# Upward products of a mixture of experts on 32-row strips of the TensorE array

## The reference

```python
probs = softmax(einsum('bsd,de->bse', x, gate_w) + gate_b)
topk_vals, topk_idx = jax.lax.top_k(probs, 2)
mask = sum(one_hot(topk_idx, 4), axis=-2)
masked = probs * mask / (sum(probs * mask, axis=-1, keepdims=True) + 1e-09)
h = gelu(einsum('bsd,edh->ebsh', x, w1) + b1)      # 96 -> 384 units, 4 experts
y = einsum('ebsh,ehd->ebsd', h, w2) + b2           # 384 units -> 96
out = einsum('bse,ebsd->bsd', masked, y)
```

## Time and profile before

| what | value |
|---|---|
| runs shown | 1208.01, 1211.01, 1211.23 us; median 1211.01 |
| profiled execution, own time | 1204.52 us |
| its span, first to last instruction | 1202.7 us |
| around the span | 1.8 us |
| mean granted clock of TensorE | 0.962 of full |
| TensorE busy | 1083.8 us, 90% of the span |
| VectorE, ScalarE, GpSimd busy | 58%, 44%, 33% |
| experts' own part | from about 1045 us to the end |

### The profile page before, as it was taken

The page is one execution under the profiler, slowest core; times in us unless marked ns, Lnnn a source line. Parts: engine busy times, 40 slices in busy tenths (PEclk is TensorE's granted clock), DMA queues, the critical chain, the costliest instruction groups (busy, mean ns, idle before and its releaser), DMA issues. The chain is left out here.

```text
span 1202.7 us, 26997 instructions
## 1 busy us (share of the span) xinstructions
PE 1083.8 (90%) x10561; PEld 708.1 (59%) x10561; DVE 702.9 (58%) x2003; ACT 525.4 (44%) x855; POOL 395.2 (33%) x616
## 2 busy tenths in 40 slices
PE   5999988899989799999999996888888978899998
PEld 2677655577745567676666664455455444466665
DVE  3899734687734466666666666476455565443333
ACT  1666623466523333434343331454343422365654
POOL 4766553766364310110101111425000000336442
PEclk9999999899979899999999999888799999899999
DMA  6400000000000000000000000000000000000000
GB/s 124 88 2 2 2 2 0 1 1 2 1 1 1 1 1 1 1 2 1 1 1 1 1 1 1 1 1 2 2 2 1 2 2 2 1 8 15 9 15 14
DMA packets 28534, 9.50 MB, mean 8 GB/s; under 512 B 26689, under 2 KB 28416, under 8 KB 28416
## 3 DMA queue, kind: packets, MB, share of 16 engines
q1 hardware_dynamic: 25392, 6.95, 2.8%
q10 hardware_dynamic: 3024, 0.92, 0.4%
HBM read 6.29 MB, written 1.57 MB: 7 GB/s over the span
## 5 line engine op out<-in xcount | busy, mean ns | idle before, releaser
L164 POOL TENSOR_TENSOR ln_v<-MV,eps 128x2 f32<-128x2 f32 (+3 forms) x81 | 16.2, 200 | 407.9 <-PE bank L1141 244.7
L1203 ACT ACTIVATE fa_e<-bank 128x1024 f32<-128x1024 f32 x64 | 65.5, 1023 | 156.8 <-PE bank L1111 156.8
L1255 DVE TENSOR_REDUCE fa_z<-bank 128x4 f32<-128x1024 f32 x64 | 77.9, 1217 | 26.4 <-PE bank L1093 24.4
L137 PE MATMUL bank<-hT,e_w 96*64 96x512 f32 x384 | 91.0, 610 | 0.0
L2049 ACT ACTIVATE ex_G<-bank,e_b 128x512 f32<-128x512 f32 x96 | 64.4, 687 | 49.9 <-PE bank L137 47.2
L2121 DVE SCALAR_TENSOR_TENSOR X<-bank,ex_L,X 128x96 f32<-128x96 f32 x128 | 31.7, 310 | 91.5 <-PE bank L137 85.0
L1853 DVE TENSOR_REDUCE ca_z<-bank 128x2 f32<-128x256 f32 x96 | 48.9, 551 | 48.7 <-PE bank L1580 48.7
L137 PEld LDWEIGHTS bank<-e_w,ex_G 128*64 128x64 f32 x1536 | 67.0, 137 | 17.3 <-issue 10.6
L1111 PE MATMUL bank<-fa_a,fa_b 64*128 64x256 f32 x512 | 73.0, 404 | 1.1 <-DVE fa_a L1262 1.1
L1771 ACT ACTIVATE ca_e<-bank 128x768 f32<-128x768 f32 x48 | 38.9, 810 | 76.4 <-PE bank L1580 76.4
L167 POOL TENSOR_TENSOR ln_r<-ln_v,minus_half 128x2 f32<-128x2 f32 (+3 forms) x81 | 71.8, 886 | 0.0
(11 more groups left out here) (251 smaller groups left out, 2493.7 us busy)
## 6 DMA issues: line engine op xcount, KB each, us to landing
out_tokens<-X SPq DMA_DIRECT2D x8, 192.0 KB, 2.1
X<-in_x SPq DMA_DIRECT2D x14, 96.0 KB, 3.4
e_w<-in_L_ffn_w SPq DMA_DIRECT2D x2, 576.0 KB
bias0r<-in_L_conv_rpb_table ACTq DMA_DIRECT2D x16, 24.0 KB
m0w<-in_L_conv_mlp_w SPq DMA_DIRECT2D x2, 144.0 KB
m1w<-in_L_conv_w SPq DMA_DIRECT2D x2, 144.0 KB
f_w<-in_L_ffn_W SPq DMA_DIRECT2D x2, 142.5 KB
mixer<-in_mixer SPq DMA_DIRECT2D x1, 256.0 KB
```

Source lines behind the costliest of these rows:

```text
L137: last = pe.matmul(out[columns], weights[:, columns], moving, **flags)
L1203: act.activation(E[v % 2][:], k.banks[:, b:b + 2, :].rearrange("p i (c q) -> p i c q", c=2), ACT.Exp).then_inc(s["exp"], 1)
L1255: dve.tensor_reduce(Z[v % 2][:].rearrange("p c (i d) -> p i c d", i=2)[:, :, :, D2], k.banks[:, b:b + 2, :].rearrange("p i (c q) -> p i c ...
```

## The change

- Four chunks go up together (`up(n, i, slot)`, i = 0 to 2: a **quad**), each into its own bank. The contraction over 96 channels is cut into three strips of 32 rows. In each of three turns the four chunks use four strips of the array: chunks 0 to 2 of the quad take strips (b + turn) % 3 of rows 0 to 95, and chunk 3 the rows 96 to 127. The matmuls are 32 rows x 128 columns x 512 tokens, no longer halves.
- For chunk 3 the tokens are copied onto rows 96 to 127, three groups of 32 channels side by side (`HX`), by three DMAs per step on SP's queue (`fourth_strip`). HX lies in the feed-forward block's buffers `bf_H`, which now belong to `k.H`. The weights of each quad's fourth chunk are loaded a second time onto these rows (three DMAs more at the start).
- Within a bank, the matmul of a later turn waits for that of the turn before (`part0` to `part3`). A quad's first matmul waits for all gelus of the quad before, and for the copies.
- `G` is one buffer with eight slots; gelu and down go chunk by chunk. `down(n, i)` does a quad's four chunks one after the other, each for four token tiles.
- The order of TensorE and ScalarE goes by three quads instead of four experts. The second upward group inside causal attention is gone; its `yield` stays.

```diff
-        def up(n, e, slot):
-            for j in range(KH):
-                v = KH * e + j
-                after(pe, s["gelu"], UP * n + v + 1 - NB)
-                halves(pe, bank[v % NB], k.ew1[:, e, j * P:(j + 1) * P], k.hT[slot][:], start=True, stop=True).then_inc(s["up"], 1)
+        def up(n, i, slot):
+            pe.wait_ge(s["hT"], n + 1)
+            pe.wait_ge(s[f"hx{slot}"], 16 * KH * (n // 2 + 1))
+            after(pe, s["gelu"], UP * n + NB * i)
+            for turn in range(KH):
+                for b in range(NB):
+                    strip = (b + turn) % KH if b < KH else KH
+                    rows = slice(32 * strip, 32 * strip + 32)
+                    v = NB * i + b if b < KH else KH * i + turn
+                    moving = k.hT[slot][rows, :] if b < KH else HX[slot][rows, turn, :]
+                    if turn:
+                        pe.wait_ge(s[f"part{b}"], (KH - 1) * (QUADS * n + i) + turn)
+                    last = pe.matmul(bank[b][:], k.ew1[rows, v, :], moving, start=(turn == 0), stop=(turn == KH - 1), skip_group_check=True)
+                    last.then_inc(s["up"] if turn == KH - 1 else s[f"part{b}"], 1)
...
         for n, slot, first, last in order:
-            for e in range(EXPERTS):
...
+            for i in range(QUADS):
+                if not first or i:
+                    up(n, i, slot)
+                if i == first and not last:
+                    tokens(n + 1, 1 - slot)
+                if i:
+                    down(n, i - 1)
                 elif not first:
...
+                    down(n - 1, QUADS - 1)
+                if i == QUADS - 1 and not last:
                     gate(n + 1, 1 - slot)
...
+        def gelus(n, i):
+            v = UP * n + NB * i
+            for b in range(NB):
+                act.wait_ge(s["up"], v + b + 1)
+                after(act, s["down"], v + b - 7)
+                act.activation(G[:, (v + b) % 8, :], bank[b][:], ACT.Gelu, bias=k.eb1[:, (NB * i + b) // KH, (NB * i + b) % KH:(NB * i + b) % KH + 1]).then_inc(s["gelu"], 1)
...
+            for i in range(QUADS):
+                if not first or i:
+                    gelus(n, i)
+                if i == first and not last:
                     tokens(n + 1, 1 - slot)
-                if e == 2 + first and not last:
+                if i == 1 + first and not last:
                     exps(n + 1, 1 - slot)
...
+        def fourth_strip(n):
+            sp.wait_ge(s["hT"], n + 1)
+            after(sp, s["up"], UP * (n - 1))
+            for g in range(KH):
+                sp.dma_start(HX[n % 2][C:P, g, :], k.hT[n % 2][32 * g:32 * g + 32, :]).then_inc(s[f"hx{n % 2}"], 16)
```

More of the change, by code:

```diff
@@ L218 @@
 CA_SEMS = LN_SEMS + "init cmask pad T hT ab abe vt v sc nm zt aug st exp av otr rec nrm ote pj oc bt"
-EX_SEMS = LN_SEMS + "T hT gl gate exp up gelu down acc g3 g4 g5 st"
+EX_SEMS = LN_SEMS + "T hT hx0 hx1 gl gate exp part0 part1 part2 part3 up gelu down acc g3 g4 g5 st"
 def setup(k, bank, a):
@@ L337, in setup @@
     k.gb = row("b_gate", a["L3_ffn_gate_b"])
-    k.ew1 = weight("e_w1", [C, EXPERTS, HID], a["L3_ffn_w1"].rearrange("e c h -> c e h"))
+    k.ew1 = sb("e_w1", [P, EXPERTS * KH, P])
+    loads.append((k.ew1[0:C].rearrange("c (e j) h -> c e (j h)", e=EXPERTS), a["L3_ffn_w1"].rearrange("e c h -> c e h")))
+    for i in range(KH):
+        e, j = divmod(4 * i + 3, KH)
+        loads.append((k.ew1[C:P, KH * i:KH * i + KH, :], a["L3_ffn_w1"][e, :, j * P:(j + 1) * P].rearrange("(g p) h -> p g h", p=32)))
     k.eb1 = weight("e_b1", [P, EXPERTS, KH], a["L3_ffn_b1"].rearrange("e (k p) -> p e k", p=P))
@@ L1328, in binary_ffn @@
     hT = sb("hT", [C, GT * P])
-    H = [sb(f"H{i}", [P, KH, GT * P]) for i in range(2)]
+    H = k.H
     Z = sb("Z", [P, GT, C])
@@ L1930, in experts @@
     UP = EXPERTS * KH
+    QUADS = UP // NB
     def sb(name, shape, dt=F32):
@@ L1939, in experts @@
     tmp = [sb(f"tmp{i}", [P, 4, C]) for i in range(2)]
-    G = [sb(f"G{i}", [P, KH, 512]) for i in range(2)]
+    G = sb("G", [P, 8, 512])
+    HX = [t[:, :, 0:512] for t in k.H]
     full = [P, 4, EXPERTS]
@@ L1992, in gate, with down @@
             last.then_inc(s["gl"], 1)
-        def up(n, e, slot):
-            for j in range(KH):
-                v = KH * e + j
-                after(pe, s["gelu"], UP * n + v + 1 - NB)
-                halves(pe, bank[v % NB], k.ew1[:, e, j * P:(j + 1) * P], k.hT[slot][:], start=True, stop=True).then_inc(s["up"], 1)
[L2000 to L2008, removed]
+        def up(n, i, slot):
[12 more added lines that the diff above has]
+                    last.then_inc(s["up"] if turn == KH - 1 else s[f"part{b}"], 1)
+        def down(n, i):
+            for b in range(NB):
+                v = NB * i + b
+                e, j = divmod(v, KH)
+                u = EXPERTS * n + e
+                pe.wait_ge(s["gelu"], UP * n + v + 1)
+                if j == 0:
+                    after(pe, s["acc"], 4 * (u - 1))
+                for t in range(4):
+                    last = halves(pe, bank[4 + e % 2][:, t * C:(t + 1) * C], G[:, (UP * n + v) % 8, t * P:(t + 1) * P], k.ew2[:, e, j, :],
+                                  start=(j == 0 and t == 0), stop=(j == KH - 1), skip_group_check=True)
+                last.then_inc(s["down"], 1)
         tokens(0, 0)
@@ L2016, in tensor @@
         yield
-        up(0, 1, 0)
         yield
         for n, slot, first, last in order:
-            for e in range(EXPERTS):
[L2021 to L2024, removed]
+            for i in range(QUADS):
[5 more added lines that the diff above has]
+                    down(n, i - 1)
                 elif not first:
[L2026 to L2029, removed]
+                    down(n - 1, QUADS - 1)
+                if i == QUADS - 1 and not last:
                     gate(n + 1, 1 - slot)
-        down(steps - 1, EXPERTS - 1)
+        down(steps - 1, QUADS - 1)
     def scalar(act):
@@ L2116, in accumulate @@
                 dve.wait_ge(s["gate"], GATE * (n + 1))
-            dve.wait_ge(s["down"], u + 1)
+            dve.wait_ge(s["down"], KH * (u + 1))
             after(dve, s["acc"], 4 * u)
@@ L2143, in sync @@
         dst = out.rearrange("b (y i) c d -> (i c) (b y) d", y=2)
+        def fourth_strip(n):
[3 more added lines that the diff above has]
+                sp.dma_start(HX[n % 2][C:P, g, :], k.hT[n % 2][32 * g:32 * g + 32, :]).then_inc(s[f"hx{n % 2}"], 16)
+        fourth_strip(0)
+        fourth_strip(1)
         for n in range(steps):
+            if n + 2 < steps:
+                fourth_strip(n + 2)
             sp.wait_ge(s["acc"], 4 * EXPERTS * (n + 1))
@@ L2167, in build @@
                 k.sems(name, sems)
+            k.H = [k.sb(f"bf_H{i}", [P, KH, GT * P], F32, own) for i in range(2)]
             ex = experts(k, bank, own, out)
```

## The result

The changed kernel takes 1257.88 us (median of four runs, 1254.38 to 1259.04), the kernel before, in the same series, 1210.44. The ratio is 1.0391 [1.0365, 1.0416]: 3.9% slower, some 47 us. The profiled execution took 1257.76 us, its span 1255.9, the mean granted clock 0.941.

The account below looks back on a forecast made before the run. TensorE was taken to set the pace. Strips 7, idle 29, clock 17 and small things 2 gave +55 us on the profiled 1204.52, so 1259.5; on the median's footing 1266, stated as 1265, range 1234 to 1290.

Parts of the forecast that it names:

- The idle behind the gate: Steps 1 to 6: TensorE waits for logits, exponential, table load and four gelus, 4.9 us each, +29 us.
- The clock: After each of six idles, about 6.5 us at half clock, 2.8 us lost each time, +17 us.
- Rival 1: Experts stage: the stall is there but the clock holds; 1248 us, chance 0.14.
- rival 5: Experts stage: clock stays at half for most of each step; 1300 us, chance 0.05.
- The strips: Upward quads: 3.71 us against 3.43 with turn waits and shape changes, 0.28 more, 24 times, about +7 us.
- change of turn: Upward quad: matmuls wait for the turn before, 0.27 signal plus 0.11 load, 0.38 each, two per quad, 0.76 us.
- changes of shape: Between row strips and column halves on TensorE: 0.11 plus 0.05 one way, 0.11 and 0.11 back, 0.38 per quad.
- Small things: Copies and weight loads nearly free; step 1's table load 0.6 us once, and the hand-over 1.4; together +2 us.
- the hand-over: From causal attention to experts: TensorE now waits until ScalarE has made its copies, 1.4 us.
- rival 4: Upward products: four strips don't run at once; 1333 us, or 1284 by the Trainium skill's 3.07; chance 0.06.
- Rivals 2 and 3: Former: exponential doesn't hold up TensorE, turns almost gapless, 1190 at best, 0.05. Latter: no stall, turn and shape costs, 1220, 0.04.

Follow-up runs that it names:

- the last kernel: Changed kernel with gate one quad earlier, each chunk on one strip, second upward quad inside causal attention, step 1's experts ranked earlier: 1194.07 us, ratio 0.9892.
- the kernel with the trap: Kernel before, no strips, gate moved behind down(1) and exponential in front of expert 2's gelus: 1229.83 us, ratio 1.0197.

## Why the prediction was right

**The direction and the range.** 1265 was forecast, 1257.88 came, within 1234 to 1290. The mechanism was the one described; the terms were a little too large. One of the signs named for it did not come: the two passes of a turn start 0.54 us apart in the changed kernel (1101.08 and 1101.62), where 0.43 was said.

**The idle behind the gate** (forecast 6 x 4.9 = 29 us): 4.75, 4.76, 4.86, 4.76, 4.76 and 4.76, 28.7 in all, in steps 1 to 6 and in no other. Its pieces were rows of the kernel before and came back the same: exponential 0.22, table 1.28, four gelus 2.42. This is why the term was good to 2%: only the signals between the engines, 0.25 us of it, were estimates. The forecast counted from the end of the gate's stream and the trace from the end of its run-out, 0.15 later; on one footing it is 4.91 against 4.9. The Trainium skill, "ScalarE: Activation LUTs", section "What ACT_TABLE_LOAD costs", gives 1283 ns for the load and 1380 more for a drain with each change of tables; the first agrees (1.28), the second isn't there (the exponential ends at 1113.93, the load runs from 1113.95, the first gelu starts at 1115.24). By the Trainium skill's figures the idle would, as an estimate, have been 1.4 us longer.

**The clock** (17 us, 2.8 a step): 2.5 a step, 15 in all, by the run in which TensorE was kept busy. The 6.5 us at half that were taken were 5.25 on average; that this is near is in part luck, since the six stretches run from 3.4 to 8.45. Rival 1, the clock that holds, and rival 5, half for most of a step, are both excluded by the stretches of 3.4 to 8.45 us.

**The strips** (7 us, 0.28 a quad). The timeline of the kernel before, TensorE, the expert that ends at 1119.51:
```profile
1114.95 2.75 PE L137 MATMUL bank<-hT,e_w 96*64 96x512 f32 x12
1117.53 2.15 PE L137 MATMUL bank<-e_w,ex_G 128*64 128x96 f32 x48
```
Up and down of one expert took 4.56 us there, so four chunks 6.08; a quad is now 6.33 (1099.90 to 1106.23), 0.25 more. A change of turn costs 0.32 where 0.38 was forecast; the 0.11 of it between the passes fits the 0.11 that the forecast gave to the load, and the signal is 0.21 instead of 0.27. The change from strips to downward halves costs the same 0.32 where 0.16 was, the way back about 0.15 (2.79 us for a quad's downward products, 1103.44 to 1106.23, against 4/3 of 1.98) where 0.22 was. That the first of these is no change of shape alone is seen where no turn waits: there it is 0.10. In the changed kernel the four strips of a turn start up to 0.13 apart (the fourth's load at 1101.21, the first's matmul at 1101.08), and they end so too. So the nearness of 0.25 to 0.28 is partly luck: two changes of turn were put 0.12 too high and the changes of shape 0.09 too low. Per step only 0.55 are left of 3 x 0.25, since tokens and gate, which took 19.42 - 4 x 4.56 = 1.18, now take 19.97 - 3 x 6.33 = 0.98. Over eight steps 4.4 us, not 7.

**Small things** (2 us): the hand-over is 1.29 where 1.4 was forecast; the table load of step 1 was not taken apart. The three copies a step cost nothing, as forecast: no idle of the changed kernel waits for them. With nine of them step 1 waited, 1.77 us and then 0.37.

**The sum.** 28.7 + 15 + 4.4 + 1.3 = 49.4 us by the parts as measured, 47.4 by the medians, 55 by the forecast. The step of the forecast that was furthest off in us is the strips (2.6), then the clock (2).

**Strips at once** (rival 4): yes, at the full rate. The forecast took the row of causal attention over the output projection and over the 3.07 for four row strips that the Trainium skill gives ("TensorE: Matmul & The Clock Gate", "Measured speedup vs the span model"). With passes 0.43 apart on four strips, as far apart as on halves, the row was the right guide; by the Trainium skill's 3.07 they would, as an estimate, be 0.56 apart. In the changed kernel itself the wait between turns hides this. Why the output projection issues more slowly was not tried.

**Rivals 2 and 3** fell with the idle. Of the 21 us that rival 2 had at the best, the last kernel reaches 12.3 by the medians (1206.41 to 1194.07) and 14.7 by the stage (168.10 to 153.44): much of the gain was there, and it was the turn waits and the order that kept it away. Most of the rest lies in the quads: even without waits between turns an upward part takes 2.79 us instead of 2.57, and the downward products behind it 2.79 instead of 2.64.

## What to carry to other kernels

When work is regrouped, go through each engine's list in the order written and ask of every instruction whether what it waits for now stands behind something that waits for it; here one gate product behind the wrong part, and an exponential of 0.2 us waiting for it in front of four gelus, were 37 of 47 us. Accumulate into one bank from the same strip and let the array keep the order, instead of going round the strips with a semaphore: the copies that this needs lay hidden on an idle queue in every step but one (1.77 us there, 0.37 in the last kernel), and 0.32 us per turn did not. An idle of TensorE costs more than its length: here half as much again, in the clock that follows.

## What the runs showed of the hardware that was not expected

- Where ScalarE has two waits in front of an activation that needs other tables, their order sets when the load goes out: at 1109.22, 0.02 us behind the exponential and 2.5 us before the products were done, with the wait for the products first; only after them, with 2.60 us of idle, with it second. In the kernel before, where the wait for the products also stands second, the load waits too, 0.67 us at 1116.07.
- Idles of nearly one length, 4.75 to 4.86 us, were followed by 3.4 to 8.45 us at half clock. What sets the length stayed open. In the kernel with the trap, idles of 2.03 us were followed by 3.4 us at half in four of six steps. The idle of 1.29 us at the hand-over was followed by 3.4 us at half with the gate moved, and by none in the changed kernel.
- From the second pass of a quad on, passes on one strip with new weights each time follow each other in 0.43 us, the time of their 512 columns, in the kernel with a strip for each chunk: the loads, 32 rows x 128 columns, cost nothing there.
